# A transformer megakernel: projections with the head dimensions on partitions, stacks loaded in five transfers, unused rows zeroed by transfers

## The reference

```
q, k, v = heads(ln(x) @ Wq + bq), heads(ln(x) @ Wk + bk), heads(ln(x) @ Wv + bv)
q, k = q * cos + rotate_half(q) * sin, k * cos + rotate_half(k) * sin
```

```
def global_latent_attn(x, ...):              # x = rmsnorm(layernorm(h), norm1_w)
    latent = x @ w_kv_down                   # 32 wide
    q, k, v = heads(x @ wq), heads(latent @ w_k_up), heads(latent @ w_v_up)
    q, k = qk_norm(rope(q)), qk_norm(rope(k))   # qk_norm: q / sqrt(mean over 8 dims + 1e-6)
    ... causal attention over 2048 rows, residual
def local_gqa_attn(x, ...):                  # the same, k and v from x, window of 32
```

## Time and profile before

| | |
|---|---|
| median of 3 runs | 1997.41 us (1994.26 to 2005.65) |
| the profiled execution | 2008.18 us, its span 2006.2 us |
| granted TensorE clock, mean of the span | 0.911 |
| PE busy | 1719.5 us, 86% |
| VectorE, ScalarE, POOL busy | 983.5, 827.8, 309.5 us |
| stages of the change | `p1_` 69.1 us, `n2_` 10.3 us, `gp_` 71.7 us, `lp_` 65.0 us |

### The profile page before, as it was taken

The page is one execution under the profiler, slowest core; times in us unless marked ns, Lnnn a source line. Parts: engine busy times, 40 slices in busy tenths (PEclk is TensorE's granted clock), DMA queues, the critical chain, the costliest instruction groups (busy, mean ns, idle before and its releaser), DMA issues. The chain is left out here.

```text
span 2006.2 us, 25536 instructions
## 1 busy us (share of the span) xinstructions
PE 1719.5 (86%) x8894; PEld 922.6 (46%) x8894; DVE 983.5 (49%) x2344; ACT 827.8 (41%) x1297; POOL 309.5 (15%) x455
## 2 busy tenths in 40 slices
PE   7688894589999889699889999997869984789998
PEld 2334563234443556244444455665623332455665
DVE  5655236778775323411351014446653438774444
ACT  5354233246667323212132224221468874654221
POOL 1112331122322323100210004000100001014000
PEclk9788997699999899899989999999579996899999
DMA  3623101301100310000000003552021001312553
GB/s 80 250 56 133 54 22 38 125 2 50 45 30 2 133 49 22 24 0 0 1 0 0 0 27 71 122 125 64 20 78 32 30 1 48 107 33 64 129 120 89
DMA packets 52620, 114.15 MB, mean 57 GB/s; under 512 B 8307, under 2 KB 34547, under 8 KB 47703
## 3 DMA queue, kind: packets, MB, share of 16 engines
q1 hardware_dynamic: 50032, 107.55, 19.3%
q0 software_dynamic: 2432, 5.00, 0.7%
q10 hardware_dynamic: 39, 0.07, 0.0%
HBM read 86.14 MB, written 19.96 MB: 53 GB/s over the span
## 5 line engine op out<-in xcount | busy, mean ns | idle before, releaser
L970 PE MATMUL psum<-f_h,w 128*128 128x512 f32 (+1 forms) x512 | 223.4, 594 | 8.6 <-ACT f_h L941 6.2
L1746 DVE TENSOR_REDUCE a_most<-psum 128x1 f32<-128x512 f32 (+3 forms) x304 | 182.1, 656 | 44.0 <-PE psum L1596 30.6
L1708 ACT ACTIVATE a_probs<-psum 128x512 f32<-128x512 f32 (+1 forms) x304 | 155.6, 578 | 99.2 <-PE psum L1626 98.5
L2540 ACT ACTIVATE t_silu<-psum 128x512 f32<-128x512 f32 x136 | 81.2, 597 | 243.6 <-PE psum L2598 242.6
L2615 PEld LDWEIGHTS psum<-t_slot,t_hid 128*128 128x128 f32 x1024 | 132.0, 191 | 55.8 <-issue 49.7
L970 PEld LDWEIGHTS psum<-f_h,w 128*128 128x128 f32 x512 | 96.0, 190 | 131.7 <-issue 118.9
L1993 ACT ACTIVATE ga_probs<-psum 128x1024 f32<-128x1024 f32 (+2 forms) x160 | 138.3, 952 | 23.4 <-PE psum L1909 23.2
L2711 DVE TENSOR_TENSOR t_prod<-t_silu,psum 128x512 f32<-128x512 f32 x104 | 71.6, 688 | 137.3 <-ACT t_silu L2540 137.3
L2615 PE MATMUL psum<-t_slot,t_hid 128*128 128x128 f32 x1024 | 134.4, 277 | 2.9 <-DVE t_hid L2702 2.9
L2598 PE MATMUL psum<-xnT,t_slot 128*128 128x512 f32 x256 | 131.6, 596 | 3.1 <-ACT t_silu L2540 3.1
L2603 PE MATMUL psum<-xnT,t_slot 128*128 128x512 f32 x256 | 130.7, 592 | 0.0
(11 more groups left out here) (377 smaller groups left out, 2932.9 us busy)
## 6 DMA issues: line engine op xcount, KB each, us to landing
t_spread<-factors SPq DMA_DIRECT2D x64, 512.0 KB, 6.4
m_experts<-experts_dram SPq DMA_DIRECT2D x14, 768.0 KB, 10.4
c_halves<-xnT SPq DMA_DIRECT2D x48, 128.0 KB, 2.3
t_slot<-experts_dram SPq DMA_DIRECT2D x32, 192.0 KB, 5.2
a_qs<-scratch_q SPq DMA_DIRECT2D x48, 96.0 KB
a_ks<-scratch_k SPq DMA_DIRECT2D x24, 192.0 KB
ga_qs<-scratch_q SPq DMA_DIRECT2D x48, 96.0 KB
la_qs<-scratch_q SPq DMA_DIRECT2D x48, 96.0 KB
```

Of the source, the lines that this page charges most:

```text
L970: ins = pe.matmul(core.psum[:, HID[n % 2], :], w(name, i * HT + j), src, start=(i == 0), stop=(i == HT - 1))
L1708: act.activation(probs[:, (n * BLOCKS + b) % PROBS, h0:h0 + heads, 0:wide], src, ACT.Exp, scale=SCALE).then_inc(probs_ready, 1)
L1746: v.tensor_reduce(most[:, row, h0:h0 + heads, qt % KPH], src, AX.X, ALU.max).then_inc(max_read, 1)
```

## The change

- **`p1_` with dimensions on partitions.** PE multiplies the weights (128 columns of q or k, straight or with the halves turned) with 512 tokens of `xnT`, so the result stands as the stacks want it, and no head is transposed. The tables and biases, which lie with tokens on partitions, are widened by eight copies on ScalarE, turned by 16 + 4 transposes on PE and copied to SBUF once, at the start. VectorE then has 512-wide operations on a whole chunk; the values are four 128-wide matmuls into one bank.
- **Stacks.** Parts of q are spilled one at a time in a layout with the parts next to each other, four transfers a chunk instead of two; a group's queries come back as two transfers of 72x2048, its keys as three: five instead of nine. Two stacks are loaded ahead instead of three.
- **Blanks.** The rows 72 to 127 are zeroed by two DMAs from the tile of zeros, issued first in the stage and awaited at its end.
- **`n2_` is gone.** `gp_` normalises `x` itself: with mean m and variance v the RMS norm of the layer norm is (x - m) / sqrt(v + eps(1e-5, 1e-6)), so its constant is `LN_EPS * EPS` and its factor `1 + EPS`. The rows that the residual needs come from 16 activations on ScalarE with bias `shift` and scale `rise`, behind its other work.
- **`gp_` and `lp_` in another order.** The products of chunk c+1 and the rests of chunk c-1 are put between the steps of chunk c; the square of the heads moves from VectorE to ScalarE; PE projects chunk c+2 before it turns chunk c.

The core of the diff:

```diff
     def load(self, sp, n):
...
         for half in range(HALVES):
-            load_queries(sp, self.scratch, n, lambda i: self.qs[part_rows(i), slot, half, :, :].rearrange("r h t -> r (h t)"), half, sem)
+            q = self.scratch[0][b, half, g, :, :, :].rearrange("i (d h) t -> (i d) (h t)", h=GROUP)
+            sp.dma_start(self.qs[0:parts * parts * HD, slot, half, :, :].rearrange("r h t -> r (h t)"),
+                         q.unsqueeze(1).broadcast_to([parts * HD, parts, GROUP * CH])).then_inc(sem, 16)
...
     def sync_all(self, sp):
         half = NC // NB
+        self.stacks.blank(sp, self.k.zero, self.blanked)
...
-        sp.wait_ge(self.blanked, 2)
         self.stacks.load(sp, 0)
         for c in range(half, NC):
-            for i in range(2):
-                self.sync(sp, c, i)
+            self.sync(sp, c)
             if c < NC - 1:
-                for n in range(1, AHEAD):
+                for n in range(1, self.stacks.ahead):
                     self.stacks.load(sp, n)
+        sp.wait_ge(self.blanked, 2 * 16)
...
 def rope_project_stage(core, w3, w3_in, v_all, stacks, tag):
...
+            for c in range(NC):
+                pe.wait_ge(ln.xnT_ready, c + 1)
+                for n, (i, turned) in enumerate(ORDER):
+                    if c:
+                        pe.wait_ge(qk_read, 4 * (c - 1) + n + 1)
+                    block_of = 2 * turned + i
+                    pe.matmul(core.psum[:, qk_bank(i, turned), :], w("qk")[:, block_of * P:(block_of + 1) * P], core.xnT[:, c * CH:(c + 1) * CH],
+                              start=True, stop=True).then_inc(qk_pe, 1)
...
+            def turn(c, n):
...
+                v.scalar_tensor_tensor((cosed, sined)[turned][:, i, :], core.psum[:, qk_bank(i, turned), :], bias[:, 2 * turned + i:2 * turned + i + 1],
+                                       table[:, turned, at:at + CH], ALU.add, ALU.mult).then_inc(qk_read, 1)
...
 def gqa_project_stage(core, w5, w5_in, v_all, stacks, kind, tag):
...
+            for c in range(NC):
+                if c + 2 < NC:
+                    project(c + 2)
+                turn(c)
...
             for c in range(NC):
...
+                v.tensor_tensor(hc, cosed[:, :, :], sined[:, :, :], ALU.add).then_inc(summed, 1)
+                if c + 1 < NC:
+                    products(c + 1, (0, 1))
+                v.wait_ge(squared, c + 1)
                 s.chain(v.tensor_reduce(per_head(mean[:, :, :]), by_head(square[:, :, :]), AX.X, ALU.add))
                 v.tensor_scalar(mean[:, :, :], mean[:, :, :], 1.0 / HD, EPS, ALU.mult, ALU.add).then_inc(mean_ready, 1)
-
+                if c + 1 < NC:
+                    products(c + 1, (2, 3))
+                if c:
+                    rest(c - 1, 1)
                 v.wait_ge(root_ready, c + 1)
...
-        norm_stage(core, "n2_")
```

More of the change, by code:

```diff
@@ L1107, with __init__ @@
     GUARDS = slice(96, 96 + PARTS)
[L1109 to L1110 removed]
+    def __init__(self, core, ctx, tag, sems, scratch, rows, key_shape, ring, ahead):
+        self.scratch, self.ring, self.ahead = scratch, ring, ahead
         self.spilled, self.stack_in = sems
@@ L1289, in _ @@
-            for t in range(NT):
-                pe.wait_ge(ln.xnT_ready, t // TPC + 1)
-                if t >= 2:
-                    pe.wait_ge(biased, 2 * (t - 1))
-                xt = core.xnT[:, t * P:(t + 1) * P]
-                for bank, name, n in ((QK_BANK, "qk", QK), (V_BANK, "v", D)):
-                    ins = pe.matmul(core.psum[:, bank[t % 2], 0:n], xt, w(name), start=True, stop=True)
-                ins.then_inc(qk_pe, 1)
-                if t:
-                    turn(t - 1)
@@ L1299, in _ @@
-            turn(NT - 1)
+            pe.wait_ge(table_ready, 2)
+            for c in range(NC):
[6 more added lines that the diff above has]
+                              start=True, stop=True).then_inc(qk_pe, 1)
+                if c >= 2:
+                    pe.wait_ge(v_ready, c - 1)
+                for t in range(TPC):
+                    ins = pe.matmul(core.psum[:, V_BANK[c % 2], t * P:(t + 1) * P], core.xnT[:, c * CH + t * P:c * CH + (t + 1) * P], w("v"), start=True, stop=True)
+                ins.then_inc(v_pe, 1)
@@ L1348 @@
+            rest(NC - 1, 1, Q)
+            values(NC - 1)
+            rest(NC - 1, 1, K)
+            rest(NC - 1, 2, Q)
+            rest(NC - 1, 2, K)
 KT = T // P
@@ L1510, in maximum @@
                     sp.dma_start(dst, most_parts[:, half, p, :]).then_inc(max_in[half], 16)
+            for n in range(stacks.ahead, RING):
+                stacks.load(sp, n)
             stacks.landed(sp, NC)
-            for n in range(AHEAD, RING):
-                stacks.load(sp, n)
             for n in range(GROUPS):
@@ L1875, in _ @@
         def _(sp):
-            stacks.landed(sp, NC)
-            for n in range(AHEAD, GROUPS):
+            for n in range(stacks.ahead, GROUPS):
+                if n == GPB:
+                    stacks.landed(sp, NC)
                 if n >= RING:
@@ L2820, in _ @@
-            turn(NC - 1)
+            ln.tensor(pe, 0)
+            ln.tensor(pe, 1)
+            down(0)
+            ln.tensor(pe, 2)
+            down(1)
+            ln.tensor(pe, 3)
+            project(0)
+            down(2)
+            down(3)
+            project(1)
+            for c in range(NC):
+                if c + 2 < NC:
+                    project(c + 2)
+                turn(c)
         @block.scalar
         def _(act):
-            stacks.blank(act, core.zero, sp_.blanked)
@@ L2842, in _ @@
+            for p in range(Split.PARTS):
+                part(NC - 1, p)
         @block.vector
```

393 lines of the change are left out of this document (221 added, 172 removed).

## The result

The changed kernel takes 1971.8 us (median of 4, 1968.0 to 1973.6), the kernel before 2000.5 in the same comparison (1994.3 to 2005.7): the ratio is 0.9854, with a 95% interval of 0.9826 to 0.9882. That is 28.7 us faster; I had forecast 45.4, and the time lies above my range. The profiled execution took 1968.03 us.

A forecast was written before the change was run, and what follows sets the result against it. Bounds, stage by stage: VectorE then SP's queue in `p1_`, PE at 0.50 in `gp_`, VectorE in `lp_`. −23 − 10.3 − 0.6 − 11.8 = −45.7 from 2008.18 gives 1962.5, scaled to 1952 us; range 1938 to 1968.

The forecast's parts named there:

- tail of `p1_`: End of `p1_`, SP's queue: last spill no longer waits, next stage at 364.2 against 387.8; 23 us used for the stage.
- four-row spill: Query spill of 4x32x512 in `p1_`: on 4 engines 4.9 us where 16 take 1.2; costed at nothing in the sum.
- Head of `p1_`: Start of `p1_`: zeros leave ScalarE, tables are turned; VectorE's first turn at 332.4 against 334.04, gain 1.6 us.
- Body of `p1_`: Chunks of `p1_`: VectorE 6.8 us a chunk at the higher clock level; last part at 362.0 instead of 380.05.
- rival D: `p1_`: PE stays at a granted 0.50, 8.9 us a chunk instead of 6.8; +7 us, 1959; 12%.
- Rival B: SP's stack loads: a transfer's issue grows with its rows, about 5 us on each of three stages' tails; 1967; 12%.
- Rival E: Blanks in `p1_`, `gp_`, `lp_` land too late if run on a single engine; about +120 us, near 2115; 3%.
- `n2_`: The stage goes, −10.3 us; its normalised rows are made in ScalarE's idle time of `gp_`.
- `gp_`: First product 12 us in, not 17.8, but PE at 0.50 bounds the stage: 71.1 us, −0.6.
- rival C: `gp_`: PE stays at a granted 1.00; −12 us, 1940; 13%.
- `lp_`: VectorE's steps between heads total 24.9 us instead of 32.8; start, chunk 0 and SP's tail also shorter; −11.8 us.
- Attention: Attention stages: five issues instead of nine, but PE waits for no stack, and the third stack loads there; 0 us.

## Why the prediction was wrong

The direction and the places were right, and the step that failed is the tail of `p1_`: "I cost it at nothing in the sum and at 1 us in the range, since SP has room behind chunk 2". The four-row spill was the term, SP had no room, and the spill cost 5.8 us; the rest of the missing time is SP's order in both tails and the start and first chunk of `lp_`.

- **Head of `p1_`.** Forecast 13.7 us to the first turn, measured 12.9. Right but for 0.8 us.
- **Body of `p1_`.** Forecast 29.6 us from there to the last part, measured 29.8. Right in its prices: a turn lasts 0.74 us, but the next operation starts 0.66 behind it, as I had it, and the clock was granted at 1.00 from 13.5 to 37.4 us in, so rival D didn't come.
- **Tail of `p1_`.** Forecast 2.2 us from the last part to the next stage, measured 11.3. 5.8 of the 9.1 are the form of the query spill, shown by two kernels that change it in different ways. The others I mis-sized in the order of SP's queue: chunk 2's spills can't go out before the first load has been issued (37.8 us in, in the run with 32-row spills), the second load follows them at 40.6, so chunk 3's start at 44.4, where I had 42.3. That rests on the timelines, and the run with one stack ahead bears it out.
- **Rival B** (an issue whose price grows with its rows) had about 5 us for each of three tails and named the right place, but not the mechanism. A 72-row load was issued in 0.8 us, with exceptions of up to 2.1 behind spills. What grew was the issue of whatever came while earlier transfers were in flight: the spill of k, a load, or a query spill itself.
- **Rival E** (the blanks land too late) didn't come: the DMA share in `p1_` falls from 0.55 in the window from 330 to 0.16 in the one from 334, 19 us after the blanks' issue.
- **`n2_`.** Forecast 10.3, measured 10.3, and its rows are free in `gp_` as far as one execution shows.
- **`gp_`.** Forecast 71.1, measured 71.4, partly by luck. I had PE at 0.50 throughout and a bare wait for banks. In fact the clock was at 1.00 for 11.6 us, all within the first 22, so rival C didn't come either. I put the latents of four chunks at 3.4 us for the lower level; those of two took 3.60 there. And they held back chunk 1's products, for which I had no term; moving them gave 4.2 us in one execution, though `gp_` varies by that much.
- **`lp_`.** Forecast 53.2, measured 59.0. The steps between chunks were right (7.8, 9.0, 7.9 against 7.9, 9.1, 7.9). The start came 12.2 us in and not 11.1; the first chunk took 10.0 us and not 8.2, because PE hands out all four tiles 1.17 us apart there and, above all, the products of chunk 1 stand ahead of the first multiply, 1.9 us that I had left out of this chunk; from the last multiply to the end it took 12.1 and not 9.1. There SP's queue ends the stage; the two runs with other spills put 1.3 and 0.5 us of it down to their form. Moreover I gave most of the gain to the interleaving, and the old order with the new stacks has 3.0 to 4.4 of the 6.0.
- **Attention.** `a1_` is 2.0 shorter and `la_` 1.4 longer. I had 0 for both, and no run settles why.
- **Where the term was lost:** I read from the trace that the nine-transfer loads run on half of the engines, wrote what four would cost, and then let SP's slack cover it without adding up SP's queue.

Left open: the 3.4 us in the last experts. The kernel before and the one with only the stacks' part need 212.9 us from there to the end, the others 209.5 to 210.6. No run was made for it.

## What to carry to other kernels

Merging transfers so that fewer are issued is worth what the queue's owner is late, but look at the shape on both sides: here a form that left four rows as the outer dimension cost `p1_` more at the queue than the issues saved. Add up the queue of the engine that ends the stage, item by item, with what each waits for, as for a compute engine; slack that "should be there" is where a hidden term lands. And run each part of a restructuring alone: here the stacks and their transfers, not the reordered arithmetic, had half or more of the gain in `lp_`.

## What the runs showed of the hardware

- The issue of a DMA on SP isn't a fixed price. Beside query spills of 4 x 32 x 512, a spill of k of the same shape took 0.37, 1.40 and 2.94 us, and two 72-row loads 1.65 and 2.94; beside spills of 32 rows these took 0.37 to 0.90, and 1.66 to 1.68. A smaller stretch comes without four-row spills too: in the kernel before one 24-row load in the second stack took 1.30 us, where the median is 0.65.
- Alone, a spill of 4 x 32 x 512 kept the DMA share at 0.25 or less, at 86 GB/s, and two in flight at 0.27 or less. The 128 KB of one took 1.8 us from the first packet to the last, those of a spill of 32 rows 0.5.
- A load of 72 rows was issued in 0.76 to 0.81 us (medians by tile) where one of 24 rows took 0.65: three times the rows for at most a quarter more.
- Two zero fills of 56 partitions, 2.75 MB together, were issued in 1.9 us, and no engine's wait shows them; with them on ScalarE `p1_` was 9.6 us longer.
- Eight kernels with the changed order of `gp_` and the same arithmetic in it took 67.7 to 72.4 us. The five with the granted clock at 1.00 for 10.2 to 11.8 us of the stage took 70.5 to 72.4, the three with 15.0 to 16.5 took 67.7 to 70.2. Gains of 1 or 2 us there can't be told from one execution.
